# Softmax sums by VectorE instead of TensorE, and one projection a round, in a gated attention kernel

## The reference, cut to what matters

```python
xn = layernorm(x)
# 16 heads of width 64
Q, K, V = xn @ Wq, xn @ Wk, xn @ Wv
attn = softmax(Q @ (K / 8).T, over keys)
s = xn + gelu(attn @ V) @ Wpost
g = silu(mx_fp6_roundtrip(xn) @ mx_fp6_roundtrip(weight).T + bias)
out = x + s * g
```

## Time and profile before

| | |
|---|---|
| time, median of 3 runs | 1434.59 us (1433.44 to 1434.7) |
| the profiled execution: its time | 1434.44 us |
| its span | 1432.7 us |
| PE busy | 1403.4 us, 98% |
| POOL busy | 1150.7 us, 80% |
| DVE busy | 1023.3 us, 71% |
| ACT busy | 805.9 us, 56% |
| granted TensorE clock, mean | 0.996 of full speed |

### The profile page before, as it was taken

The page is one execution under the profiler, slowest core; times in us unless marked ns, Lnnn a source line. Parts: engine busy times, 40 slices in busy tenths (PEclk is TensorE's granted clock), DMA queues, the critical chain, the costliest instruction groups (busy, mean ns, idle before and its releaser), DMA issues.

```text
span 1432.7 us, 26455 instructions
## 1 busy us (share of the span) xinstructions
PE 1403.4 (98%) x10066; PEld 756.4 (53%) x10066; DVE 1023.3 (71%) x1377; ACT 805.9 (56%) x1123; POOL 1150.7 (80%) x549
## 2 busy tenths in 40 slices
PE   5899999999999999999999999999999999999998
PEld 3455555555555555555555554555555455555488
DVE  6777777777777777777777777777777777777432
ACT  2455675555556566555556666555556555555573
POOL 1588888888888888888888888888888888888930
PEclk9999999999999999999999999999999999999999
DMA  2011112111111111111111111111111110221471
GB/s 79 16 39 61 46 60 68 54 46 46 61 47 55 58 54 59 47 61 47 60 54 54 46 50 57 54 52 54 54 46 46 47 46 31 68 75 50 159 242 40
DMA packets 66833, 85.50 MB, mean 60 GB/s; under 512 B 26906, under 2 KB 40986, under 8 KB 66708
## 3 DMA queue, kind: packets, MB, share of 16 engines
q1 hardware_dynamic: 66708, 83.83, 18.0%
HBM read 68.34 MB, written 15.45 MB: 58 GB/s over the span
## 4 chain that ended last, share of the span: by engine, by line
PE 96%; DVE 2%; ACT 1%; POOL 1%; issue 0%; DMA 0%; SPq 0%; POOLq 0%; ACTq 0%
PE acc L512 31%; PE scores L493 24%; PE peaks L472 12%; PE extra L385 8%; PE scores L502 6%; PE extra L417 5%; PE extra L398 4%; PE scores L576 4%; DVE half_maxes L947 1%; PE extra L441 1%; POOL prob_sum L832 1%; PE extra L434 0%; PE extra L408 0%; DVE half_maxes L974 0%; PE scores L408 0%
## 5 line engine op out<-in xcount | busy, mean ns | idle before, releaser
L832 POOL TENSOR_TENSOR prob_sum<-prob_sum,probs 128x1024 f32<-128x1024 f32 x384 | 914.3, 2381 | 179.5 <-ACT probs L698 146.6
L947 DVE TENSOR_REDUCE half_maxes<-peaks 128x2 f32<-128x1024 f32 x504 | 616.5, 1223 | 313.9 <-PE peaks L472 310.6
L698 ACT ACTIVATE probs<-scores 128x1024 f32<-128x1024 f32 x357 | 354.9, 1023 | 405.1 <-PE scores L502 403.9
L512 PE MATMUL acc<-probs,vals 128*64 128x512 f32 x2048 | 486.3, 596 | 0.7 <-ACT raw L684 0.7
L512 PEld LDWEIGHTS acc<-probs,vals 128*64 128x64 f32 x2048 | 138.6, 137 | 243.4 <-issue 218.9
L472 PE MATMUL peaks<-k_hi,q_hi 64*128 64x512 f32 x1008 | 229.0, 448 | 3.8 <-DVE half_maxes L947 3.4
L493 PE MATMUL scores<-q_hi,k_hi 64*128 64x512 f32 x1024 | 203.7, 393 | 0.0
L493 PE MATMUL scores<-q_hi,k_lo 64*128 64x512 f32 x1024 | 202.3, 390 | 0.0
L493 PE MATMUL scores<-q_lo,k_hi 64*128 64x512 f32 x1024 | 202.0, 389 | 0.0
L472 PEld LDWEIGHTS peaks<-k_hi,q_hi 64*128 64x128 f32 x1008 | 95.2, 183 | 194.1 <-issue 89.2
L984 DVE TENSOR_TENSOR probs<-scores,max_rep 128x1024 f32<-128x1024 f32 x155 | 188.3, 1215 | 4.6 <-PE scores L493 4.6
(11 more groups left out here) (157 smaller groups left out, 1000.4 us busy)
## 6 DMA issues: line engine op xcount, KB each, us to landing
max_rep<-max_scratch SPq DMA_DIRECT2D x62, 512.0 KB, 3.6
inv_sum<-inv_scratch SPq DMA_DIRECT2D x124, 128.0 KB, 2.9
att_scratch<-att SPq DMA_DIRECT2D x48, 256.0 KB, 2.0
probs<-att_scratch SPq DMA_DIRECT2D x8, 512.0 KB, 7.6
max_scratch<-turned SPq DMA_DIRECT2D x252, 1.0 KB
xTs<-att_scratch SPq DMA_DIRECT2D x4, 512.0 KB, 4.7
out_dram<-xn SPq DMA_DIRECT2D x8, 256.0 KB, 2.3
max_rows<-max_scratch SPq DMA_DIRECT2D x126, 2.0 KB
```

Source lines behind the costliest of these rows:

```text
L512: last = mm(acc[own[h], :], vals[(s // 2) % 2][:, j, own[h]], probs[j][:, h, :], start=(k == 0), stop=(k == KT - 1), tile_position=col[h])
L698: sa.activation(probs[j][:, :, :], src[:, :, :], ACT.Exp, scale=DH ** -0.5).then_inc(probs_ready, 1)
L832: gp.tensor_tensor(prob_sum[s % 2][:, :, :], before[:, :, :], probs[order(s)[j]][:, :, :], ALU.add).then_inc(probs_summed, 1)
L947: v.tensor_reduce(half_maxes[:, :, f // 2, f % 2], peaks[:, :, :], AX.X, ALU.max).then_inc(peaks_read, 1)
```

## The change

The fill `den` is gone from TensorE. In its place VectorE reduces `prob_sum` with a transposing reduction (`fold_sums`): each block of 32 keys x 32 queries is transposed and summed over its keys, which leaves 4 partial sums (one per 32 partitions) for each of 2 x 512 queries in 128 x 32 values; a 32 x 32 transposition turns them for a contiguous store. They come back from DRAM as 32 partitions x (4 x 32), and `invert_sums` adds the four groups and inverts. All 64 steps go this way.

The projections are spread: k, k, q, v of the next pair in the four rounds of an even step with the second v behind the last, and the first q of the pair after the next in round 3 of the odd step. `turn_x` and `ffn` move to round 0 of the odd step. Quantisation begins a round earlier. `BY_VECTOR` becomes four blocks in an even step and one in an odd; their total of 155 stays.

```diff
     def extras(s, r):
...
+        if half == 0 and n + 1 < NP:
+            if s == 0 and r == 0:
+                before.append(("q", 1, 0))
+                behind.append(("k", 1, 0))
+            else:
+                before.append((("k", n + 1, 0), ("k", n + 1, 1), ("q", n + 1, 1), ("v", n + 1, 0))[r])
+            if r == 3:
                 behind.append(("v", n + 1, 1))
+        if half == 1:
+            if r == 0 and n > 0:
+                before.append(("turn_x", n - 1))
+                behind.append(("ffn", n - 1))
...
+            if r == 1:
+                behind.append(("quant", n))
+            if r == 3 and n + 2 < NP:
+                before.append(("q", n + 2, 0))
+            if s == NS - 1 and r == 3:
+                before.append(("turn_x", n))
+                behind.append(("ffn", n))
...
-    BY_VECTOR = ((0, 4, 6), (0, 2))
+    BY_VECTOR = ((0, 2, 4, 6), (0,))
...
             def store_sums(s):
-                is_read(sp, ("den", s))
+                sp.wait_ge(folded, s + 1)
                 above(sp, sums_loaded, 16 * s)
-                for h in (0, 1):
-                    sp.dma_start(sum_d[h:h + 1, :], inv[s % 2][h * DH:h * DH + 1, :]).then_inc(sums_stored, 16)
+                sp.dma_start(sum_d.rearrange("g b i -> (g b) i"), sums_turned).then_inc(sums_stored, 16)
...
-                if s > 1 and not inverted_in_place(s - 2):
+                if s > 1:
+                    store_inverse(s - 2)
+                store_maxima(s + 1)
+                if s > 1:
                     spread_inverse(s - 2)
...
+                load_maxima(s + 1)
+                if s > 0:
                     store_sums(s - 1)
...
                     load_sums(s - 1)
...
-            def sums(use):
-                s = use[1]
-                w, filled = fill(use)
-                pe.wait_ge(probs_summed, 7 * s + 7)
-                for h in (0, 1):
-                    last = mm(w[own[h], :], ones[:, :], prob_sum[s % 2][:, h, :], start=True, stop=True, tile_position=col[h])
-                last.then_inc(filled, 1)
...
-            for use in (("den", NS - 1), ("turn_x", NP - 1), ("ffn", NP - 1)):
-                run(use)
...
-                    if j == (7, 5)[s % 2] and s > 1:
+                    if j == ((7, 5)[s % 2] if s < NS - 2 else 3) and s > 1:
                         normalise(s - 2)
...
+            def fold_sums(s):
+                dve.wait_ge(probs_summed, 7 * s + 7)
+                above(dve, inv_stored, 16 * s)
+                v.tensor_reduce(group_sums, prob_sum[s % 2][:, :, :].rearrange("p h (b i) -> p (h b) i", i=SQ), AX.X, ALU.add,
+                                apply_transpose=True).then_inc(group_summed, 1)
+                dve.wait_ge(group_summed, s + 1)
+                v.transpose(sums_turned, group_sums).then_inc(folded, 1)
+
+            def invert_sums(s):
                 dve.wait_ge(sums_loaded, 16 * (s + 1))
-                v.reciprocal(sums_flat[:, :], sums_flat[:, :]).then_inc(flat_inverted, 1)
+                v.tensor_reduce(sums_flat, sums[0:SQ, :].rearrange("b (g i) -> b i g", g=P // SQ), AX.X, ALU.add).then_inc(combined, 1)
+                dve.wait_ge(combined, s + 1)
+                v.reciprocal(sums_flat, sums_flat).then_inc(flat_inverted, 1)
```

More of the change, by code:

```diff
@@ L40, in extras @@
         before, behind = [], []
[L41 to L51, removed]
-                behind.append(("v", n + 1, 1))
-            if r == 1 and n == 0:
+        if half == 0 and n + 1 < NP:
[5 more added lines that the diff above has]
+            if r == 3:
+                behind.append(("v", n + 1, 1))
+        if half == 1:
+            if r == 0 and n > 0:
+                before.append(("turn_x", n - 1))
+                behind.append(("ffn", n - 1))
+            if r == 0 and n == 0:
                 before.append(("w",))
             if r == 1 and n % HP in (4, 5) and n // HP + 1 < B:
[L56 to L60, removed]
+                before.append(("x", n // HP + 1, n % HP - 4))
+            if r == 1:
[5 more added lines that the diff above has]
+                behind.append(("ffn", n))
         return before, behind
@@ L139, in gated_attention_kernel @@
         stats = sb("stats", [P, 6, B, NB])
-        eps, spare = sb("eps", [P, 1]), sb("spare", [P, 1])
-        exponent = sb("exponent", [P, 1])
+        small = sb("small", [P, 3])
+        eps, spare, exponent = (small[:, k:k + 1] for k in range(3))
         quant = [sb(f"quant{z}", [P, D]) for z in (0, 1)]
@@ L214, in high_number @@
             name, n, half = use
[L215 removed]
+            return 4 * n + 1 + ([("q", 0), ("k", 0), ("q", 1), ("k", 1)] if n == 0 else [("q", 0), ("k", 0), ("k", 1), ("q", 1)]).index((name, half))
         def above(eng, s, value):
@@ L337, in _ @@
             sp.wait_ge(pv_done, KT * (NS - 2))
-            for p in range(HP, HP + 5):
-                load_att(p)
+            load_att(HP)
+            store_sums(NS - 2)
+            load_att(HP + 1)
+            load_sums(NS - 2)
+            load_att(HP + 2)
+            store_inverse(NS - 2)
+            load_att(HP + 3)
+            spread_inverse(NS - 2)
+            load_att(HP + 4)
             sp.wait_ge(scores_ready, KT * NS)
@@ L718, in _ @@
                 for r in range(4):
+                    if r == 0 and ahead and half == 1:
+                        copy_v(("v", n + 1, 1))
                     exps(s, 2 * r)
@@ L760, in _ @@
                             root(part_of(later, 0))
-                        if half == 1 and r > 1 and n % HP == 3:
-                            scale_rows(later, r - 2)
+                        if half == 0 and r < 2 and n % HP == 4:
+                            scale_rows(later, r)
             for p in range(HP):
@@ L977, in subtract_maxima @@
             def subtract_maxima(s, j):
-                if j == 0:
+                if not any(by_vector(s, i) for i in range(j)):
                     dve.wait_ge(rep_loaded, 16 * s)
@@ L1016, in _ @@
                 ahead, later = n + 1 < NP, n // HP + 1
-                even = half == 0 and ahead
                 for r in range(4):
@@ L1044, in _ @@
                         turn_squares(1)
-                    if r > 1 and half == 1:
-                        quantise_tile(n, 2 * r - 3)
-                    if r == 0 and s > 1 and not inverted_in_place(s - 2):
-                        invert_flat(s - 2)
-                    if r == 2 and s == NS - 1:
-                        for c in range(4):
-                            invert(NS - 2, c)
+                    if half == 1 and r in (1, 2):
+                        quantise_tile(n, 2 * r - 2)
+                    if not (FOLD_FIRST and half == 1 and s < NS - 1) and r == (FOLD_AT[half] if s < NS - 1 else 1) and s > 0:
+                        fold_sums(s - 1)
+                    if r == 3 and s == NS - 1:
+                        invert_sums(NS - 2)
                     if s == 0 and r == 3:
```

159 lines of the change are left out of this document (73 added, 86 removed).

## The result

The changed kernel took 1390.09 us (median of 4, 1389.51 to 1390.66) beside 1434.64 us (1433.44 to 1435.92) for the kernel before: a ratio of 0.9689 with the interval 0.9673 to 0.9706. Forecast were 1389 us. The profiled execution took 1389.97 us with a span of 1388.2, against 1434.44 and 1432.7.

A forecast was written before the change was run, and what follows sets the result against it. TensorE, 98% busy, was taken as the bound. Savings of 27.6 us (24 pairs), 10.9 (6 pairs), 0.9 (pair 0) and 5.9 (the end), 45.3 off 1434.44, gave 1389 us; 8-in-10 range 1372 to 1414.

The forecast's parts named there:

- `den` at 0.91 us each, 39.54 us a pair of TensorE's own: Removing two den fills a pair saves TensorE 1.82 us, taking its own work from 41.36 to 39.54 us.
- The wait of odd round 1: VectorE's chain behind the second peak ends late, so TensorE waits 0.67 us in each of 24 pairs.
- Fold at 1.21 us: VectorE's transposing reduction costs the same as a plain one from SBUF, 1.21 us, with 2.17 kept as upper case.
- odd round 3 without cover: VectorE's work ends at 6.05 us against 5.91 available; no loss taken, but no cover left.
- even round 3 with 0.8: VectorE's work with the fold ends at 5.62 us in a round of about 5.9: fits with 0.8 us to spare.
- Way through DRAM: Sums stored and loaded back in 4.0 us, 0.8 in hand before the tightest inversion, so VectorE does not wait.
- The end: Fewer den fills and waits in the last steps, and turn_x and ffn moved forward, save 5.9 us together.
- the six intervals with a fill of x: Six pairs with a later batch's x transposed in odd round 1 cover the wait: 1.82 us each, 10.9 in all.
- Rival 1: TensorE alone decides and the odd round 1 wait does not come: 16 us more gained, 1373 us; chance 0.15.
- Rival 2: Fold or way back through DRAM takes longer: 1423 us with a 2.17 us fold, 1406 at half; chance 0.20.
- rival 3: The transposing reduction passes over its data several times and the change loses: 1509 us at three passes; chance 0.05.
- rival 4: GpSimd becomes the bound, its work grown by 14% to 41.0 us a pair: 1417 us; chance 0.03.

The follow-up runs named there:

- e1: The changed kernel with the odd step's inversion of the returned sums moved from round 1 to the end of round 0: 1380.67 us, ratio 0.9626.
- e6: The kernel before, with its den matmuls over 64 of 512 columns and everything else in place: 1394.53 us, ratio 0.9724.
- e2: The changed kernel with the transposing reduction (fold) done twice in each odd step: 1427.81 us, ratio 0.9955.
- e3: The changed kernel with the transposing reduction (fold) done twice in each even step: 1405.01 us, ratio 0.9801.
- e8: e1 with ScalarE's subtraction of means for a later batch moved from even round 3 to odd round 2, its squares to odd round 3: 1375.37 us, ratio 0.9590.
- e5: The kernel before with VectorE's folds in place of den; order of projections, subtractions and quantisation as before: 1422.83 us, ratio 0.9919.
- e4: The changed kernel with VectorE's subtractions as before, blocks 0, 4, 6 in even and 0, 2 in odd steps: 1416.80 us, ratio 0.9878.
- e7: e1 with the square root for a later batch's x one step later and what follows it one or two steps later: 1380.45 us, ratio 0.9624.

## Why the prediction was right

The forecast was 45.3 us off, measured were 44.5. By its own steps:

- **`den` at 0.91 us each, 39.54 us a pair of TensorE's own.** Right: 39.59 with the wait taken away (e1), 0.74 for seven eighths of the columns (e6).
- **The wait of odd round 1.** Right in place, chain and operand (e1 takes it away and gains 9.4 us), too large in size: 0.42 to 0.48 instead of 0.67. The second reduction starts 2.61 us into its round and the late one 5.63, where I had 2.68 and 5.98. The chain between them is 3.02 us, where I added 3.30 and took off 0.08. The way to the transposition of maxima takes 2.00 us instead of 2.10, although the small reduction costs 0.36 instead of 0.28; quantisation starts 0.08 us behind the transposition instead of 0.21, since it doesn't wait for it; and its three steps take 0.94 instead of 0.99.
- **Fold at 1.21 us, odd round 3 without cover, even round 3 with 0.8.** Right for the steady pair: 1.235 us; e2 pays all, e3 0.13 of 1.2. The prediction never asked what stood in even round 3 of the pairs that prepare a batch's x; in the changed kernel no peak waits for it, only e3 shows it.
- **Way through DRAM.** Right for this kernel: of 64 inversions only 2 waited for a DMA, for 10.4 us in all, both in the last 70 us, where TensorE's matmuls show no wait. SP's store and load were 1.43 us apart (1.41 taken). The load moves 16 KB and landed 1.7 us after its issue, where I took 2.6 from a load of 4 KB: 3.1 us in all instead of 4.0.
- **The missed term.** Pairs 2, 10 and 18 (intervals 3, 11 and 19) saved 0.25 us each, where the sum had 1.15: ScalarE's eight subtractions of means stand in front of the copy of `vals`, for which TensorE now waits (e8). That is 4.6 us of waits, and the sum had nothing for it.
- **The end.** Forecast were 5.9 us and 1.15 for the last full pair, 7.05 in all; measured 8.8. Of these the tail, from the first output projection on, has 5.2 (66.2 to 61.0 us), where I had 3.15. In e5, whose tail still has `turn_x` and `ffn` but no `den`, it is 63.3 us: `den` is worth 2.9 there, and the two small fills with their hand-overs 2.3. The rest of the surplus is open.

Put together, the number is closer than its terms, and that is luck:

```
                                         forecast  measured
start and interval 1                       +0.9      -1.35
the six intervals with a fill of x        +10.9     +10.55
intervals 3, 11, 19                        +3.45     +0.75
the twenty others up to 30                +23.0     +25.8
from interval 31 on                        +7.05     +8.8
in all                                     45.3      44.5
```

The wait of odd round 1 was put too high, by 2.8 us over the twenty intervals, and the end 1.75 too low; the missed wait for `vals` and the start, with its lower clock, took as much away again and 0.8 us more.

Rival 1 (no wait, 1373 us) is out for the changed kernel; e8 at 1375 shows that nearly its time was there to be had. Rival 2 falls with the fold's 1.235 us and with a way back that no mid-run inversion waited for (in e5, with its other places, 14 did), rival 3 with the fold, rival 4 with additions that stayed at 2.38.

## What to carry to other kernels

Work taken from the engine that sets the time is worth its duration only where the engine that takes it over is free when it is waited for: e5 kept a quarter of the gain, the same folds with other places all of it, and two more steps put in holes gave another 14.7 us. Count the cover round by round, the rare rounds too: the ones that prepare the next batch were wrong here in e3, in e4 and in the forecast. And number the intervals of a table as the program numbers its rounds, or an experiment like e7 edits the wrong place. Where the distance between two of the bound engine's instructions grows, the bracket that names the wait shows only a part of it.

## What the runs showed of the hardware

A transposing reduction of 128 x 1024 elements costs 1235 ns, against 1209 for a plain one. A reduction of 32 x 128 elements in groups of four that lie 32 apart costs 359 ns, where one of 128 x 128 elements in groups of 32 neighbours costs 280. What stands behind a peak reduction of 1.23 us and waits for nothing starts 1.13 to 1.15 us behind the start of it (61 folds in the kernel after), and what reads its result 1.25 to 1.27 us behind (the joining of maxima). GpSimd's additions of 128 x 1024 elements took 2382 ns with 64 folds beside them.
